# Two buffers of normalised rows, and row scatters issued in groups of four, two and two

## What is computed

```
x = x + gnn(layernorm(x), adj)         # two convolutions over the nodes (the second with 17 taps),
                                       # relu(h + x); A = exp(-dist(s, s)) * adj, A @ relu(x @ w_msg);
                                       # a GRU cell over both
x = x + ffn(layernorm(x))              # mixture of experts, on each of the 8192 nodes alone:
    xn     = layernorm(x) * gamma + beta
    logits = xn @ Wr + br              # 8 experts
    top 2 of 8, weights = softmax of the two logits
    y      = sum over both experts e of w_e * (gelu(xn @ W1[e] + b1[e]) @ W2[e] + b2[e])
```

## Time and profile before

| | |
|---|---|
| median of 3 timed runs | 665.62 us (665.16 to 666.0) |
| the profiled execution | 662.19 us |
| its span, first to last instruction | 660.4 us |
| mean granted TensorE clock | 0.99 |
| DMA queue of SP (hardware) | 83.27 MB, 40.1% of 16 engines |
| DMA queue of POOL (software) | 16.92 MB, 16.6% |
| row scatters (L1008) | 112, 117.2 us busy on POOL |
| halves of adds (L973) | 96, 160.1 us busy on POOL |

### The profile page before, as it was taken

The page is one execution under the profiler, slowest core; times in us unless marked ns, Lnnn a source line. Parts: engine busy times, 40 slices in busy tenths (PEclk is TensorE's granted clock), DMA queues, the critical chain, the costliest instruction groups (busy, mean ns, idle before and its releaser), DMA issues.

```text
span 660.4 us, 12858 instructions
## 1 busy us (share of the span) xinstructions
PE 618.4 (94%) x3784; PEld 530.3 (80%) x3784; DVE 498.9 (76%) x2050; ACT 418.0 (63%) x824; POOL 345.9 (52%) x273
## 2 busy tenths in 40 slices
PE   2899999999999994999999999999999987999996
PEld 2779788787979794797979797979797966888874
DVE  6968899988989792797979797979797964533322
ACT  3654546485858473585858585858585846666763
POOL 2200405245656384666666665757575644356772
PEclk9998999999999996999999999999999999999999
DMA  8427131718397838147474747474737578963352
GB/s 289 149 79 277 58 121 52 245 56 245 70 348 194 228 76 238 31 130 185 119 195 110 204 110 203 93 218 95 221 71 228 149 156 225 270 152 49 52 82 46
DMA packets 93413, 101.01 MB, mean 153 GB/s; under 512 B 7664, under 2 KB 71920, under 8 KB 93040
## 3 DMA queue, kind: packets, MB, share of 16 engines
q1 hardware_dynamic: 70752, 83.27, 40.1%
q0 software_dynamic: 22592, 16.92, 16.6%
HBM read 75.85 MB, written 30.51 MB: 161 GB/s over the span
## 4 chain that ended last, share of the span: by engine, by line
PE 62%; DMA 10%; DVE 9%; POOL 6%; issue 6%; ACT 5%; POOLq 1%; SPq 0%; DVEq 0%; ACTq 0%
DMA out<-y_t,xt 8%; PE G L703 7%; PE Y L593 7%; PE C L527 5%; PE C L525 5%; PE C L526 5%; PE G L525 4%; PE G L593 4%; POOL out L973 4%; PE G L527 4%; PE G L526 4%; POOL routed L1008 2%; PE Y L601 2%; PE M L531 2%; PE C L697 2%
## 5 line engine op out<-in xcount | busy, mean ns | idle before, releaser
L973 POOL DMA_INDIRECT out<-y_t,xt x96 | 160.1, 1668 | 129.4 <-DMA out<-y_t,xt 96.4
L1008 POOL DMA_INDIRECT routed<-row,at_u x112 | 117.2, 1046 | 120.4 <-DVE at_u L1202 90.2
L525 PE MATMUL C<-cv_h,w_hi 128*128 128x256 f32 (+1 forms) x432 | 131.7, 305 | 1.6 <-DVE cv_l L1063 1.1
L527 PE MATMUL C<-cv_h,w_lo 128*128 128x256 f32 (+1 forms) x432 | 125.1, 290 | 0.0
L526 PE MATMUL C<-cv_l,w_hi 128*128 128x256 f32 (+1 forms) x432 | 124.9, 289 | 0.0
L525 PEld LDWEIGHTS C<-cv_h,w_hi 128*128 128x128 f32 x432 | 83.4, 193 | 4.0 <-issue 2.2
L526 PEld LDWEIGHTS C<-cv_l,w_hi 128*128 128x128 f32 x432 | 83.2, 193 | 1.3
L527 PEld LDWEIGHTS C<-cv_h,w_lo 128*128 128x128 f32 x432 | 83.1, 192 | 0.6
L593 PE MATMUL Y<-ge,w_t 128*128 128x256 f32 x228 | 59.2, 382 | 1.4 <-ACT ge L798 0.8
L703 PE MATMUL G<-ex,msg_t 128*128 128x512 f32 x128 | 58.9, 603 | 0.3 <-ACT gh L896 0.3
L798 ACT ACTIVATE ge<-H,w_t 128x256 f32<-128x256 f32 x114 | 47.8, 472 | 5.4 <-PE H L570 3.4
(11 more groups left out here) (264 smaller groups left out, 1692.4 us busy)
## 6 DMA issues: line engine op xcount, KB each, us to landing
w_t<-w_all SPq DMA_DIRECT2D x66, 392.0 KB, 4.7
adj<-adj_t SPq DMA_DIRECT2D x16, 1024.0 KB, 5.6
xt<-routed SPq DMA_DIRECT2D x66, 144.0 KB, 3.8
x_ln<-x SPq DMA_DIRECT2D x16, 256.0 KB, 2.9
x_res<-x SPq DMA_DIRECT2D x16, 256.0 KB
wd<-w_all SPq DMA_DIRECT2D x10, 392.0 KB, 4.2
out<-x SPq DMA_DIRECT2D x15, 256.0 KB
w_all<-w_s SPq DMA_DIRECT2D x1, 3136.0 KB, 11.4
```

Source lines behind the costliest of these rows:

```text
L525: pe.matmul(psum, hi(w), rhs_h, start=start, stop=False)
L527: return pe.matmul(psum, lo(w), rhs_h, start=False, stop=stop)
L973: nc.gpsimd.indirect_dma_start(out=out, out_offset=bass.IndirectOffsetOnAxis(ap=xt[j][:, t, R_ID:R_ID + 1].bitcast(U32), axis=0), in_=y_t[ ...
L1008: nc.gpsimd.indirect_dma_start(out=routed, out_offset=bass.IndirectOffsetOnAxis(ap=at_u[:, n:n + 1], axis=0), in_=row[:, n // TOP, :], in_ ...
```

## The change

`row` and `at_u` become two tiles each, used in turn by the graph's number; `rows_out` becomes two semaphores, one per buffer. ScalarE writes the rows of graph d when the scatters of graph d - 2 have landed. On POOL six of the eight scatters of a graph stay in its iteration (four behind `tile_add(1)`, two behind `tile_add(2)`); the last tile's two are issued in the next iteration, behind `tile_add(-1)`. SP's waits ask for the same graphs as before, over both semaphores. POOL clears both row tiles at the start.

```diff
-        row = sb("row", [P, NT, ROW])
+        rows = [sb(f"row{i}", [P, NT, ROW]) for i in range(2)]
...
-        at_u = sb("at_u", [P, NT * 2], U32)
+        ats_u = [sb(f"at_u{i}", [P, NT * 2], U32) for i in range(2)]
...
+        rows_out = [sem(f"rows_out{i}") for i in range(2)]
...
-                    sp.wait_ge(rows_out, 16 * NT * TOP * (g - 1))
+                    for i in range(2):
+                        sp.wait_ge(rows_out[i], 16 * NT * TOP * ((g - i) // 2))
...
-                if d > 0:
-                    act.wait_ge(rows_out, 16 * NT * TOP * min(d, ROUTED))
+                if d > 1:
+                    act.wait_ge(rows_out[d % 2], 16 * NT * TOP * (d // 2))
                 else:
-                    act.wait_ge(zeroed, 2)
+                    act.wait_ge(zeroed, 3)
...
-                def rows_to_experts(a, b):
+                def rows_to_experts(d, a, b):
                     for n in range(a * TOP, b * TOP):
                         nc.gpsimd.indirect_dma_start(
-                            out=routed, out_offset=bass.IndirectOffsetOnAxis(ap=at_u[:, n:n + 1], axis=0),
-                            in_=row[:, n // TOP, :], in_offset=None).then_inc(rows_out, 16)
+                            out=routed, out_offset=bass.IndirectOffsetOnAxis(ap=ats_u[d % 2][:, n:n + 1], axis=0),
+                            in_=rows[d % 2][:, n // TOP, :], in_offset=None).then_inc(rows_out[d % 2], 16)
...
                 tile_add(-1)
+                if 0 < d <= ROUTED:
+                    rows_to_experts(d - 1, NT - 1, NT)
                 tile_add(0)
                 tile_add(1)
                 if tail and d < ROUTED:
                     pool.wait_ge(rt_step, router_first(d) + ROUTER_STEPS)
-                    rows_to_experts(0, NT // 2)
+                    rows_to_experts(d, 0, NT // 2)
...
                 tile_add(2)
                 if tail and d < ROUTED:
-                    rows_to_experts(NT // 2, NT)
+                    rows_to_experts(d, NT // 2, NT - 1)
...
-            nc.gpsimd.memset(row[:], 0.0).then_inc(zeroed, 1)
+            for i in range(2):
+                nc.gpsimd.memset(rows[i][:], 0.0).then_inc(zeroed, 1)
```

More of the change, by code:

```diff
@@ L304, in gnn_moe @@
         pads_stored = sem("pads_stored")
-        x_ln_loaded, x_res_loaded, adj_loaded, out_set, rows_out = map(
-            sem, ("x_ln_loaded", "x_res_loaded", "adj_loaded", "out_set", "rows_out"))
+        x_ln_loaded, x_res_loaded, adj_loaded, out_set = map(
+            sem, ("x_ln_loaded", "x_res_loaded", "adj_loaded", "out_set"))
+        rows_out = [sem(f"rows_out{i}") for i in range(2)]
         pe_xnT, pe_xT, pe_conv1, pe_s, pe_msg, pe_router, pe_dist, pe_rank, pe_conv2, pe_msgT = map(
@@ L493, in _ @@
                 sp.dma_start(routed[bass.ds(at, TILE), :], pads[0:TILE, :]).then_inc(pads_stored, 16)
-            sp.wait_ge(rows_out, 16 * NT * TOP * ROUTED)
+            for i in range(2):
+                sp.wait_ge(rows_out[i], 16 * NT * TOP * ((ROUTED + 1 - i) // 2))
             sp.wait_ge(pads_stored, 16 * (EXPERTS + 3))
@@ L679, in iteration @@
                     pe.wait_ge(exp_done, NT * g + 3)
-                    row_transposes(G0, row, NT).then_inc(pe_xnT, 1)
+                    row_transposes(G0, rows[d % 2], NT).then_inc(pe_xnT, 1)
                 if is_graph(g, 0):
@@ L767, in _ @@
                     pe.wait_ge(xn_ready, g + 1)
-                    row_transposes(C2, row, NT).then_inc(pe_xnT, 1)
+                    row_transposes(C2, rows[g % 2], NT).then_inc(pe_xnT, 1)
                 if i == AT_ROUTE:
@@ L810, in normalized_rows @@
                 act.wait_ge(nb_done, d + 1)
-                if d > 0:
-                    act.wait_ge(rows_out, 16 * NT * TOP * min(d, ROUTED))
+                if d > 1:
+                    act.wait_ge(rows_out[d % 2], 16 * NT * TOP * (d // 2))
                 else:
-                    act.wait_ge(zeroed, 2)
+                    act.wait_ge(zeroed, 3)
                 for t in range(NT):
-                    last = nc.scalar.activation(row[:, t, 0:P], x1_of(d)[:, t, :], ACT.Identity, scale=rs[:, t:t + 1],
+                    last = nc.scalar.activation(rows[d % 2][:, t, 0:P], x1_of(d)[:, t, :], ACT.Identity, scale=rs[:, t:t + 1],
                                                 bias=nb[:, t:t + 1])
@@ L1193, in place @@
                                                  over(w12s, 2, [P, NT * 2, EXPERTS]), ALU.mult))
-                    step(nc.vector.tensor_tensor(row[:, :, R_W:R_W + EXPERTS], hot_w[:, :, 0, :], hot_w[:, :, 1, :],
+                    step(nc.vector.tensor_tensor(rows[d % 2][:, :, R_W:R_W + EXPERTS], hot_w[:, :, 0, :], hot_w[:, :, 1, :],
                                                  ALU.add))
-                    step(nc.vector.tensor_copy(row[:, :, R_ID].bitcast(U32), tid[:]), wait=False)
+                    step(nc.vector.tensor_copy(rows[d % 2][:, :, R_ID].bitcast(U32), tid[:]), wait=False)
                     dve.wait_ge(pe_rank, d + 1)
@@ L1201, in place @@
                                                  hot_w[:, :, :, :].rearrange("p t k e -> p (t k) e"), AX.X, ALU.add))
-                    step(nc.vector.tensor_copy(at_u[:], at_f[:].rearrange("p t k -> p (t k)")), wait=False)
+                    step(nc.vector.tensor_copy(ats_u[d % 2][:], at_f[:].rearrange("p t k -> p (t k)")), wait=False)
                     assert done[0] == ROUTER_STEPS
@@ L1506, in _ @@
             w_lo_part("conv_s")
-            dve.wait_ge(zeroed, 2)
+            dve.wait_ge(zeroed, 3)
             first(0)
```

## The result

The changed kernel took 655.82 us (median of 4 runs, 653.9 to 656.33), the kernel before 665.39 beside it (4 runs, 662.88 to 666.0). The ratio is 0.9858, with a 95% interval of 0.9825 to 0.9891: 9.6 us faster. The forecast was 653.2 us. The profiled execution took 653.9 us with a span of 652.1. Lines have moved by three to six: L905 is now L908, L816 L819, L536 L539, L973 L976, L1008 L1011, VectorE's product L1408 is L1414.

The account below looks back on a forecast made before the run. TensorE, busy 94% of the span, was taken as the bound. Removing 12.2 us of row stalls takes the 665.62 us median to 653.4; 0.2 of the 3.4 us excess gives 653.2, range 649.5 to 658.5.

Parts of the forecast that it names:

- The wait and its removal: ScalarE's waits to write `row`, iterations 6 and 7: two buffers remove both, 0.79 + 11.43 = 12.2 us with the clock loss.
- The root: POOL's queue: SP's large pad stores in iteration 5 delay one add's landing, making POOL and later row scatters late.
- the sum: The prediction's reckoning of queue times and gains: 12.2 us off the span, 660.4 to 648.2 us.
- 0 to 2.5 us given back in iteration 7: Moved scatters land late, so TensorE may wait for the new tile in iteration 7; 0 to 2.5 us, taken as 0.
- POOL's slack: POOL's queue, each iteration: regrouped scatters need net 1.6 us less, slack grows from 0.7 to 2.3 us; no time gained.
- The tail: Last loads behind the loop: their path holds DVE and SP, no add and no row scatter; cost 0.
- The 3.4 us: Timed median above the profiled execution: perhaps a longer stall that would go too; 0.2 taken in, mostly in stall 0.03.
- (a): Stall moves to tile loads, TensorE waiting at iteration 7's tile; 2.5 us given back, 655.9 or 658 us; chance 0.17.
- (b): Another wait, SP's tile refill after an add lands, ends at the same place; 665.6 us; 0.05 together with (d).
- (d): Buffers fail: a count one graph too high leaves ScalarE's wait as it is; 665.6 us; 0.05 together with (b).
- (c): POOL bounds every iteration through longer landings around the moved pair; slower, 669.7 us at a 35.2 us cycle; chance 0.05.

Follow-up runs that it names:

- e3: Kernel before, SP's two large pad stores issued behind the loads of iteration 3 instead of iteration 5; 651.67 us, ratio 0.9802.
- e4: Changed kernel run once more with no edit, first chip; 652.80 us, ratio 0.9828.
- The early reads: Changed kernel, SP reading registers for the first two of the last tile loads ahead of its waits; 659.03 us (ratio 0.9817), repeated on another chip 649.97 us (0.9783).
- e12: Changed kernel with early register reads and large pad stores behind the loads of iteration 3, third chip; 651.73 us, ratio 0.9802.
- e1: Changed kernel with two buffers but row scatters four and four as in the kernel before, first chip; 654.08 us, ratio 0.9885.
- e5: Changed kernel with VectorE's product of exponentials and adjacency cut to 8 of 512 columns, second chip; 661.71 us, ratio 0.9879.
- e9: Two buffers with the old scatter groups of four and four, repeated on the third chip; 654.24 us, ratio 0.9858.
- e10: Changed kernel run again with no edit, third chip; 652.24 us, ratio 0.9814.
- e2: Kernel before with one buffer, only the scatter grouping changed to four, two, two; 671.56 us, ratio 1.011.
- e11: Changed kernel with SP's early register reads for the first two of the last tile loads, third chip; 649.97 us, ratio 0.9783.
- e7: Changed kernel with early register reads and large pad stores behind the loads of iteration 3, second chip; 656.73 us, ratio 0.9812.

## Why the prediction was right, and where not

**The wait and its removal: right.** `row` was the cause, both excess distances went (0.79 forecast, 0.79 measured; 11.43 and 11.42), the clock loss went with them, and no other wait took the place. ScalarE's own work was done in time, as reckoned.

**The root: right.** e3 shows it: the same 12 us come from moving the stores. In the changed kernel the stores still delay the add (203.07; the sum had 201.71, and 1.3 us of the difference are iteration 4's). It just no longer matters.

**0 to 2.5 us given back in iteration 7: 0, as taken.** SP's first load stands at 254.03, less 1.3 for iteration 4 252.7, against 252.5. The margin was larger than reckoned. The sum had the pair done at 252.4 to 254.4; it is done at 245.86 + 1.50 = 247.4. In iteration 6 the kernel before waited 4.72 and 5.41 us for two landings; in the new order the pair lies in one of these gaps and a single wait of 3.56 us is left. The half of an add that took 3.77 us at 210.99 has a counterpart at 211.14 that takes 1.61, which no term of the sum held: here the add just missed VectorE's product, and that is luck (in e4 the same half takes 4.11).

**POOL's slack: wrong, without cost.** The step "net 1.6 us less per iteration, slack 2.3 us" failed. From iteration 10's first add to the end of the `at_u` wait it is 360.70 − 340.36 = 20.3 us, where it was 371.22 − 352.79 = 18.4; I had put 0.9 more. 0.45 more is the pair itself (346.79 − 343.86 against 2.48), 1.5 the half that takes 3.51 instead of 2.03. The new order shifts that add so that it starts inside VectorE's product. The saving at the old place was 2.3, near the 2.5 of the sum (from the first scatter behind `at_u` to the next iteration's first add, 14.65 us in iteration 9 before and 12.31 in iteration 10 now). So POOL gained 0.4 us and not 1.6, and I had read the warning and passed over it: 3.77 in the earlier trace rows, for which I gave no reason. The same shows in iteration 5: the sum had the add of 187.78 at 185.3 to 186.2, it stands at 189.35, less 1.3 for iteration 4 188.05, behind a half at 178.86 that takes 3.81 us. That the stores would not be outrun was allowed for, so it cost nothing.

**The tail: wrong, 2.1 us.** "That path holds no add and no row scatter: 0" was true of the path and false of its margin. I followed what SP waits for and not what TensorE then waits for. In the kernel before two of the last loads came just too late, with 0.40 us of wait at 545.16 and 0.88 at 548.05; I had not looked at these. In the changed one TensorE waits 1.64 and 0.43 us, 0.8 more in all, and runs at a clock of 0.82 and 0.68 in two stretches that had 1.00; that the rest of the 2.1 us is the clock's is argued from this and not measured alone. The early reads show SP's pace to be the cause of these waits. It is not shown to be the cause of the clock: e12 has 0.82 and 0.70 there without a wait for `xt`, and e3, with one buffer, 0.82 and 0.73 with a tail of 126.7 us. SP's first of these loads stands 3.7 us behind the last copy and not 3.1 as before (537.26 − 534.19). That comes with the second buffer and not with the grouping: it is 3.4 to 3.8 us in e1, e4, e5, e9 and e10, and 3.0 in e3, which has one buffer and the old groups. By what step the buffer does it is not settled.

**Iteration 4: 1.3 us that no reckoning from one trace could have.** They are absent in e4 and e10.

**The size.** On the recorded comparison the gain was 9.6 us where the sum said 12.2. Between the two profiled executions it was 8.3, which is 12.2 less 1.3, 0.4 and 2.1 to within 0.1. The changed kernel beside the one before on the first and third chip gained 11.0 and 11.7 us. The 3.4 us by which the median lay above the profiled execution were not all in the stall: in the recorded comparison they are 3.2 before and 1.9 after, each from four runs. The measured 655.8 us lie 2.6 above the forecast; the two later comparisons, in whose traces iteration 4 loses nothing, stand nearer to the 12.2.

**The rivals.** (a) has no wait for `xt` in the loop; (b) and (d) are out with the distance of 33.40; (c) with it too, for nine iterations. Without the second buffer the pair behind the first add does cost in every iteration: e2 is 7.8 us slower. But that is not the mechanism of (c). POOL does not become the bound there, it still waits 1.39 and 1.62 us for `at_u` in iterations 8 and 9; it is ScalarE that waits some 1.35 us for the moved pair before it may write `row`.

## What to carry to other kernels

Where a wait is long in one iteration only, look for what is done once near it, on any queue: the cure by a second buffer cost two tiles and a rewritten order, the cure by moving two stores one line. When such a stall is taken out, list the waits of the bounding engine over the whole span and ask of each short one how it stands once everything before it is earlier. A reordering on a full queue is to be reckoned with the place at which each instruction then lies beside other engines' work, not by medians alone.

## What the hardware showed that I had not expected

Half of an add, one indirect DMA of POOL, mostly takes 1.55 to 1.6 us on the queue, but up to 4.13 when it begins around VectorE's product of two tensors from on-chip memory. In the kernel before, POOL and then VectorE:
```profile
144.58 4.13 POOL L973 DMA_INDIRECT out<-y_t,xt  x1 [8.37 <-DVE y_t L1302]
```
```profile
144.74 2.49 DVE L1408 TENSOR_TENSOR ex<-ex,adj 128x512 f32<-128x512 f32 x4
```
All halves over 2.2 us in these two kernels stand there, two before and nine in the changed one, and each ends 1.4 to 1.5 us behind the last of VectorE's four products, whichever of the two began first; the four keep their 2.5 us. Not every DMA that meets the products is stretched: the half at 213.06 in the changed kernel begins 0.8 us into them and takes 1.91. In e4 and e10 single row scatters take up to 3.29 us in the same place, where 0.99 is their median, and end 0.9 us behind the products. With the product cut to 8 columns (e5) no half is above 2.07. The Trainium skill (SBUF — State Buffer, section Who interferes with whom) says that a VectorE instruction with two SBUF inputs contends with a GpSimd instruction that reads SBUF, and that the pair of ports the two share is locked exclusively. The lengths and e5 agree that they contend. Having begun first does not spare POOL: the add at 144.58 began 0.16 us before the products and was stretched all the same. The same section tells of a probe in which such a product did not stall a DMA, and infers a reason; these rows do not bear that out.

Megabytes on SP's queue do delay an add on POOL's: with 3.8 MB of pad stores on the way the next add still waits 4.6 us behind four scatters, without them (e3) not at all. And ScalarE or TensorE starts a single instruction around the `C` products up to 1.4 us late in some executions, with nothing in the profile to end that wait: TensorE has eight waits for `tz`, 2.8 us, in one trace (e5) and 0.2 us in each of e4, e10 and e11. In e7 it also starts one product behind the loop (L597) 2.2 us late for nothing that the profile shows.
